# One output product moved ahead of a one-hot sum, and every row gather gated, in the last stage of a mixture-of-experts kernel

## The chip, the cores and the metric

The kernel runs on one core of a Trainium2 chip. The metric is the device time of one execution in microseconds (us), and of several executions the median. Engines: TensorE (PE; PEld are its weight loads), VectorE (DVE), ScalarE (ACT), GpSimd (POOL) and SyncE (SP), which only issues transfers.

## The reference

```
x = x + attention(layernorm(x), ctx)            # 512 tokens of 256
y = layernorm(x)
topk_idx, tw = gate(y)                          # 4 of 32 experts for a token
combine = zeros(T, E).at[t, topk_idx].add(tw)
routed = sum over experts e of combine[:, e] * (silu(y @ w1[e].T) * (y @ w3[e].T)) @ w2[e].T
out = x + routed + shared_swiglu(y)
```

Only the routed part matters here.

## The kernel before

Everything before about 220 us (attention, layer norm, gate, routing tables) is untouched. In the last stage the chosen token rows stand in 32 units of two blocks of 64 rows, handled in 16 pairs j = 0 to 15. TensorE takes a pair through four steps, each in its turn of one loop over j = 0 to 18 written out by hand:

- `x_rows` (line 708) transposes the gathered rows; ScalarE copies them out (968).
- `hidden` (719) multiplies by w1 and w3, 16 matmuls. ScalarE applies silu (981), and VectorE multiplies by the other half in `gated` (1314).
- `g_rows` (729) transposes that product, two transpositions; ScalarE copies it out in `gT_evict` (975).
- `out_rows` (740) multiplies by w2, 8 matmuls.

What becomes of an output depends on the pair. Pairs 0 to 9 are written to memory (`y_rows`), and GpSimd fetches them back for each token in 16 indirect transfers, `collect` (1418), each of 128 rows; VectorE adds each fetched tile to the result in `add_rows` (1298; the very last at 1367). I number these gathers 0 to 15. Pairs 10 to 15 don't go through memory. For each of them, p = 0 to 5, ScalarE writes a weighted copy (`weighted_high`, 991), VectorE the remainder of it (`weighted_rows`, 1289) and a one-hot matrix (`hot_rows`, 1278), and TensorE sums them into the token rows in `combine(p)` (685, 16 matmuls), the last in `combine_last` (696). VectorE adds these sums at the end (`add_sum`, 1358), and SyncE stores the four tiles (448).

Each engine works through its own list in order. VectorE's, at the end, is: `add_rows` of gathers 3 to 5, `gated(15)`, `hot_rows(5)`, `weighted_rows(4)`, gathers 6 to 8, `weighted_rows(5)`, gathers 9 to 11, gathers 12 and 13, `add_sum(0)` and `(1)`, gather 14, `add_sum(2)` and `(3)`, gather 15. The one-hot matrices and the weighted copies have two buffers, so that

```
                if p >= 2:
                    dve.wait_ge(acc_mm, p - 1)
```

stands in front of `hot_rows(p)`: `hot_rows(5)` waits until `combine(3)` has ended. `combine(p)` waits for `weighted_rows(p)`, and `g_rows(j)` for `gated(j)`. ScalarE's list at the end is: `gT_evict(14)`, silu of pair 15, `weighted_high(4)`, `gT_evict(15)`, `weighted_high(5)`.

A gather can be gated: `pool.wait_ge(*gates[i])` holds gather i until a count of TensorE's steps is reached. `hu_mm`, `gt_mm`, `yu_mm` count `hidden`, `g_rows` and `out_rows`, and `acc_mm` counts `combine`.

Of the kernel before, what the change touches and what calls it, by code (L numbers as in the profile page):

```python
# [46 lines left out]
NU = E  # L47
DIR = 12
# [17 lines left out]
def build(nc, x, ctx_kv, w_attn, w_gate, gate_bias, w_exp, rope_q, rope_x, rope_kv, ident_in, iota_in, w_sh, moe_c, iota_t, xn_dram, y_dram, out):  # L66
    with ExitStack() as stack:
# [3 lines left out]
        def sem(name):  # L71
            return stack.enter_context(nc.semaphore(name))
# [209 lines left out]
        gt_mm = sem("gt_mm"); gt_ev = sem("gt_ev"); yu_mm = sem("yu_mm"); yu_ev = sem("yu_ev")  # L282
# [38 lines left out]
        def out_count(u):  # L321

            return len([s for s in USED[:u + 1] if s not in AHEAD])
# [129 lines left out]
        def _(pe):  # L453
# [219 lines left out]
            def slot_weights():  # L673
                pe.wait_ge(w_one, 1)
                for k in range(NK):
                    mm = pe.matmul(sw_ps, f(one_r[:, k, :]), w_both[:, :, k, :], start=(k == 0), stop=(k == NK - 1))
                mm.then_inc(sw_mm, 1)
# [12 lines left out]
            def combine_last(p):  # L690
                pe.wait_ge(yu_ev, NG_U // 2 + p + 1)
                pe.wait_ge(oh_done, p + 1)
                for tt in range(TT):
                    for i in range(2):
                        for hl in range(2):
                            mm = pe.matmul(acc_ps[tt // 2][:, (tt % 2) * D:(tt % 2 + 1) * D],
                                           one_hot[:, p % 2, i, tt * P:(tt + 1) * P], yd[:, p % 2, i, hl, :],
                                           start=False, stop=(i == 1 and hl == 1 and tt % 2 == 1), skip_group_check=True)
                    if tt % 2 == 1:
                        mm.then_inc(acc_end, 1)  # L700

            def x_rows(j):
                if j >= 1:
                    pe.wait_ge(xt_ev, j)
                for u in (2 * j, 2 * j + 1):
                    pe.wait_ge(d_xg[u % XG], 16 * (u // XG + 1))
                    for dc in range(ND):
                        mm = pe.transpose(xt_ps[:, (u % 2 * ND + dc) * P:(u % 2 * ND + dc + 1) * P],  # L708
                                          xg[:, u % XG, dc * P:(dc + 1) * P], ident[:, :])
                mm.then_inc(xt_mm, 1)  # L710

            def hidden(j):
                pe.wait_ge(xt_ev, j + 1)
                if j >= 2:
                    pe.wait_ge(gu_done, j - 1)
                for u in (2 * j, 2 * j + 1):
                    for dc in range(ND):
                        for s, w in enumerate((over_w[u], u * WE)):
                            mm = pe.matmul(hu_ps[j % 2][s * BLK:(s + 1) * BLK, (u % 2) * 2 * I:(u % 2 + 1) * 2 * I],  # L719
                                           xTu[:, u % XS, dc, s * BLK:(s + 1) * BLK],  # L720
                                           wall[:, bass.ds(w + dc * 2 * I, 2 * I)], start=(dc == 0), stop=(dc == ND - 1))
                mm.then_inc(hu_mm, 1)

            def g_rows(j):
                pe.wait_ge(gu_done, j + 1)
                if j >= 1:
                    pe.wait_ge(gt_ev, j)
                for i in range(2):
                    mm = pe.transpose(gt_ps[:, i * P:(i + 1) * P], gu[:, i, :], ident[:, :])
                mm.then_inc(gt_mm, 1)  # L730

            def out_rows(j):
                pe.wait_ge(gt_ev, j + 1)
                if j == 0:
                    pe.wait_ge(sh_sum, TT)
                if j >= 2:
                    pe.wait_ge(yu_ev, j - 1)
                for u in (2 * j, 2 * j + 1):
                    for s, w in enumerate((over_w[u], u * WE)):
                        mm = pe.matmul(yu_ps[j % 2][s * BLK:(s + 1) * BLK, (u % 2) * D:(u % 2 + 1) * D],  # L740
                                       gTu[:, u % GS, s * BLK:(s + 1) * BLK],
                                       wall[:, bass.ds(w + 2 * ND * I, D)], start=True, stop=True)
                mm.then_inc(yu_mm, 1)
# [70 lines left out]
            for j in range(NU // 2 + 3):  # L814
                if j == 1:
                    hidden(0)
                if j < NU // 2:
                    x_rows(j)
                if j == 1:
                    slot_weights()  # L820
                if 2 <= j < NU // 2 + 2:
                    g_rows(j - 2)
                if 2 <= j <= NU // 2:
                    hidden(j - 1)
                if j == NU // 2 + 1:
                    out_rows(j - 2)
                if j == NU // 2 + 2:
                    combine_last(DIR // 2 - 1)
                elif j - 3 >= NG_U // 2:
                    combine(j - 3 - NG_U // 2)  # L830
                if 2 <= j < NU // 2 + 1:
                    out_rows(j - 2)


# [536 lines left out]
        @block.gpsimd  # L1371
        def _(pool):
            links = [0]

            def link(ins):

                links[0] += 1
                ins.then_inc(chain_p, 1)
                pool.wait_ge(chain_p, links[0])


            pool.wait_ge(d_kv, 32)
            hd = DC // 2
            for b in range(B):
                rows = slice(b * LC, (b + 1) * LC)
                pool.tensor_tensor(kvr[:, rows, 0, :], kv[:, rows, :], kvtab[:, :, 0, :], ALU.mult)
                pool.tensor_tensor(kvr[:, rows, 1, 0:hd], kv[:, rows, hd:DC], kvtab[:, :, 1, 0:hd], ALU.mult)
                link(pool.tensor_tensor(kvr[:, rows, 1, hd:DC], kv[:, rows, 0:hd], kvtab[:, :, 1, hd:DC], ALU.mult))
            link(pool.tensor_tensor(kvr[:, :, 0, :], kvr[:, :, 0, :], kvr[:, :, 1, :], ALU.add))
            pool.tensor_copy(kvr[:, :, 1, :], kvr[:, :, 0, :]).then_inc(kv_roped, 1)  # L1390

            def ropes(g, j):
                p = NPG * g + j
                for k in range(NQT):
                    if (p, k) in BY_DVE:
                        continue
                    pool.wait_ge(wk_out, out_count(use(g, "ABC"[k], j)))
                    if (g, "ABC"[k], j) != ALONE:
                        pool.wait_ge(q_swap, TURNED.index((g, "ABC"[k], j)) + 1)
                    rope_tile(pool, link, g, j, k, 2).then_inc(rope_p, 1)  # L1400
                    await_roped(pool, p, k)

            pool.wait_ge(d_rope, 16)
            for g in range(NG):
                for j in range(NPG):
                    ropes(g, j)
            pool.wait_ge(d_moe, 16)
            pool.tensor_copy(lower_b[:, :], lower).then_inc(const_b, 1)

            def gather(u):  # L1410
                if u >= XG:
                    pool.wait_ge(xt_mm, (u - XG) // 2 + 1)
                pool.indirect_dma_start(xg[:, u % XG, :], None, xn_dram, bass.IndirectOffsetOnAxis(idx[:, u:u + 1], 0)) \  # L1413
                    .then_inc(d_xg[u % XG], 16)

            def collect(tt, k):
                i = tt * TOPK + k
                pool.indirect_dma_start(y4[:, tt, k, :], None, y_dram, bass.IndirectOffsetOnAxis(place[:, i:i + 1], 0)) \  # L1418
                    .then_inc(d_y4[i], 16)

            for tt in range(TT):
                pool.wait_ge(d_xn[tt], 16)
            pool.wait_ge(idx_done, 2)
            for u in range(XG):
                gather(u)
            for u in range(XG, NU):
                gather(u)
            pool.wait_ge(placed, 1)
            for r in range(YS // 2):
                pool.wait_ge(d_yu[r], 16 * (NG_U // YS))  # L1430
            G2 = NG_U // 2
            gates = {1: (acc_mm, 1), 2: (yu_mm, G2 + 2), 3: (hu_mm, G2 + 4), 4: (acc_mm, 2), 5: (yu_mm, G2 + 3), 6: (hu_mm, G2 + 5),
                     7: (acc_mm, 3), 8: (yu_mm, G2 + 4), 9: (hu_mm, G2 + 6), 10: (acc_mm, 4), 11: (yu_mm, G2 + 5)}
            for i in range(NK):
                if i == 0:
                    pool.wait_ge(sw_mm, 1)
                if i in gates:
                    pool.wait_ge(*gates[i])
                collect(*divmod(i, TOPK))
# [96 lines left out]
```

## Time and profile before

| | |
|---|---|
| median of 3 executions | 302.06 us (301.9 to 302.15) |
| the profiled execution | 301.82 us |
| its span, first to last instruction | 299.5 us |
| PE busy | 282.5 us (94%) |
| DVE busy | 181.4 us (61%) |
| ACT busy | 156.4 us (52%) |
| POOL busy | 129.5 us (43%) |
| mean granted TensorE clock | 0.995 |

The span is what the trace covers; the profiled execution's own time is 2.32 us longer. Shares of busy time are means over stages with different limits. The stage that the change touches is the last 20 us.

### The profile page before, as it was taken

Reading aid. Unit: us, or ns where it says so; the run is one execution under the profiler, and the core shown is the slowest. Engines: PE = TensorE matmul, PEld = TensorE weight load, DVE = VectorE, ACT = ScalarE, POOL = GpSimd, SP = SyncE. Lnnn points to the kernel's source line nnn. Section 1 sums busy time; section 2 is a strip of 40 time slices with the busy share of each in tenths; the row PEclk is TensorE's granted clock in tenths of the full one; section 3 lists DMA queues with packets and bytes.
Section 4 is the critical chain, followed back from the end, with each engine's and each line's share of the span. In section 5 each row is a group of like instructions: output and inputs, shape, how many; then the busy total and the mean of one; then the engine's idle time right before and its main releaser. Section 6 shows DMA issues by size and latency. Waiting matters only on the chain.

```text
span 299.5 us, 5458 instructions
## 1 busy us (share of the span) xinstructions
PE 282.5 (94%) x1831; PEld 202.7 (68%) x1831; DVE 181.4 (61%) x434; ACT 156.4 (52%) x373; POOL 129.5 (43%) x121
## 2 busy tenths in 40 slices
PE   8988799999999999999999999978789999999982
PEld 6857568676777666787667777754567666676662
DVE  4877776576757777765854466158842233344676
ACT  2747469675785866777773355185212333343330
POOL 0656328791036770079940000000176555565572
PEclk9999999999999999999999999999999999999998
DMA  7962500001700001600039992402033544432234
GB/s 235 402 253 79 204 1 2 0 2 25 255 3 1 0 3 46 218 0 1 2 127 380 402 352 78 173 2 70 1 106 106 150 150 144 154 109 72 70 82 130
DMA packets 15994, 34.41 MB, mean 115 GB/s; under 512 B 2528, under 2 KB 8416, under 8 KB 15968
## 3 DMA queue, kind: packets, MB, share of 16 engines
q1 hardware_dynamic: 13664, 27.77, 26.0%
q0 software_dynamic: 2304, 6.29, 7.4%
q8 instruction: 16, 0.26, 0.4%
q14 instruction: 10, 0.08, 0.1%
HBM read 30.38 MB, written 3.67 MB: 114 GB/s over the span
## 4 chain that ended last, share of the span: by engine, by line
PE 85%; DVE 7%; DMA 2%; issue 2%; ACT 2%; POOL 1%; POOLq 0%; DVEq 0%; ACTq 0%
PE bank L719 10%; PE bank L612 10%; PE bank L595 9%; PE bank L583 5%; PE bank L562 5%; PE bank L584 4%; PE bank L740 4%; PE bank L456 4%; PE bank L458 4%; PE bank L457 4%; PE bank L505 3%; PE bank L708 3%; PE bank L537 3%; PE bank L685 3%; PE bank L540 3%; PE bank L463 2%
## 5 line engine op out<-in xcount | busy, mean ns | idle before, releaser
L1413 POOL DMA_INDIRECT rope<-xn_rows,idx x32 | 31.2, 974 | 83.3 <-DVE idx L1307 61.9
L893 ACT ACTIVATE prob<-bank,nmax 128x512 f32<-128x512 f32 x48 | 32.7, 685 | 38.9 <-DVE nmax L1097 38.9
L361 POOL TENSOR_TENSOR rtmp<-abuf,rope 128x512 f32<-128x512 f32 x20 | 25.7, 1284 | 60.4 <-PE bank L458 41.0
L1097 DVE TENSOR_REDUCE nmax<-bank 128x1 f32<-128x512 f32 x64 | 41.2, 685 | 8.7 <-PE bank L584 8.4
L719 PE MATMUL bank<-wall,nmat 128*64 (+1 forms) x256 | 31.2, 386 | 0.8 <-ACT nmat L968 0.8
L612 PE MATMUL bank<-pT,kvr 128*64 128x256 f32 x256 | 31.2, 386 | 0.0
L1115 DVE COPY pT<-bank 128x512 f32<-128x512 f32 x32 | 22.0, 687 | 13.1 <-PE bank L595 12.9
L583 PE MATMUL bank<-kdup,qsp 128*128 128x512 f32 x64 | 28.3, 442 | 1.2 <-ACT prob L893 1.2
L364 POOL TENSOR_TENSOR roped<-rtmp 128x512 f32<-128x512 f32 x20 | 25.9, 1295 | 1.6
L1314 DVE TENSOR_TENSOR kv<-bank,kv 128x256 f32<-128x256 f32 x16 | 6.8, 425 | 32.5 <-ACT kv L981 32.4
L595 PE MATMUL bank<-ident,prob 128*128 128x128 f32 x192 | 26.3, 273 | 0.0
L595 PEld LDWEIGHTS bank<-ident,prob 128*128 128x128 f32 x192 | 22.6, 141 | 4.9 <-issue 1.7
L362 POOL TENSOR_TENSOR rtmp<-abuf,rope 128x512 f32<-128x512 f32 x20 | 25.8, 1292 | 0.0
L584 PE MATMUL bank<-kdup,qsp 128*128 128x512 f32 x64 | 25.3, 395 | 0.0
L719 PEld LDWEIGHTS bank<-wall,nmat 128*64 128x64 f32 x256 | 16.9, 137 | 10.5 <-issue 3.5
L612 PEld LDWEIGHTS bank<-pT,kvr 128*64 128x64 f32 x256 | 16.9, 137 | 9.8 <-issue 2.8
L902 ACT COPY pT<-bank 128x512 f32<-128x512 f32 x32 | 18.9, 592 | 7.5 <-PE bank L595 7.2
L1061 DVE COPY abuf<-bank 64x512 f32<-64x512 f32 x20 | 13.7, 684 | 14.7 <-ACT abuf L867 14.4
L968 ACT COPY nmat<-bank 128x512 f32<-128x512 f32 x16 | 9.4, 585 | 23.3 <-PE bank L708 23.3
L1418 POOL DMA_INDIRECT ctT<-y_rows,place x16 | 16.3, 1017 | 10.3 <-PE bank L719 3.7
L456 PE MATMUL bank<-xnT,msplit 128*128 128x512 f32 x46 | 20.6, 447 | 0.0
L583 PEld LDWEIGHTS bank<-kdup,qsp 128*128 128x128 f32 x64 | 12.0, 188 | 9.2 <-issue 7.4
(217 smaller groups left out, 559.8 us busy)
## 6 DMA issues: line engine op xcount, KB each, us to landing
wall<-in_w_exp SPq DMA_DIRECT2D x32, 384.0 KB, 7.5
wring<-in_w_attn SPq DMA_DIRECT2D x16, 224.0 KB, 4.3
wring<-in_w_attn SPq DMA_DIRECT2D x4, 640.0 KB, 8.1
y_rows<-nmat SPq DMA_DIRECT2D x10, 256.0 KB, 2.1
wring<-in_w_attn SPq DMA_DIRECT2D x4, 512.0 KB, 7.0
rope<-in_rope_q SPq DMA_DIRECT2D x1, 768.0 KB, 7.0
x_sb<-in_x SPq DMA_DIRECT2D x1, 512.0 KB, 3.6
xn_rows<-xn SPq DMA_DIRECT2D x4, 128.0 KB, 1.7
```

The source lines that it names most:

```text
L361: eng.tensor_tensor(t0.rearrange("p (b s) -> p b s", b=B), own.rearrange("p (b s) -> p b s", b=B), cos, ALU.mult)
L362: link(eng.tensor_tensor(t1.rearrange("p (b s) -> p b s", b=B), other.rearrange("p (b s) -> p b s", b=B), sin, ALU.mult))
L364: return eng.tensor_tensor(roped[:, j, k, :], t0, t1, ALU.add)
L456: pe.matmul(out_ap, a_hi, b_hi, start=first, stop=False)
L583: pe.matmul(s_ps[t % 3][:, :], q, kdup[:, 0, b * L:(b + 1) * L], start=True, stop=False)
L584: pe.matmul(s_ps[t % 3][:, :], q, kdup[:, 1, b * L:(b + 1) * L], start=False, stop=True) \
L595: mm = pe.transpose(t_ps[t % 2][:, lc * P:(lc + 1) * P], probs[t % 4][:, lc * P:(lc + 1) * P], ident[:, :])
L612: mm = pe.matmul(pv_ps[hh * DC:(hh + 1) * DC, 0:S], kvr[:, b * LC + lc, 0, :], pT[:, (2 * n + hh) % PR, lc, :], start=(lc == 0), stop=(lc ...
L719: mm = pe.matmul(hu_ps[j % 2][s * BLK:(s + 1) * BLK, (u % 2) * 2 * I:(u % 2 + 1) * 2 * I], xTu[:, u % XS, dc, s * BLK:(s + 1) * BLK], wall ...
L893: act.activation(probs[t % 4], s_ps[t % 3][:, :], ACT.Exp, bias=nmax[:, t:t + 1], accum_out=psum_e[:, t:t + 1]).then_inc(s_exp, 1)
L1097: dve.tensor_reduce(nmax[:, t:t + 1], s_ps[t % 3][:, :], AX.X, ALU.max, negate=True).then_inc(s_max, 1)
L1413: pool.indirect_dma_start(xg[:, u % XG, :], None, xn_dram, bass.IndirectOffsetOnAxis(idx[:, u:u + 1], 0)) \
```

## The change

`combine(3)` leaves the turn j = 16 and stands in the turn j = 17, between `g_rows(15)` and `out_rows(15)`. `out_rows(14)` thereby follows `hidden(15)` at once. No matmul, copy or transfer is added or taken away, and no other engine's list changes order. In GpSimd's list each gather from 1 to 15 has a gate; before, 12 to 15 had none. Three gates count transpositions (`gt_mm`). G2 is 10.

```diff
-                if j == NU // 2 + 1:
+                if j == NU // 2:
                     out_rows(j - 2)
-                if j == NU // 2 + 2:
+                elif j == NU // 2 + 1:
+                    combine(DIR // 2 - 3)
+                    out_rows(j - 2)
+                    combine(DIR // 2 - 2)
+                elif j == NU // 2 + 2:
                     combine_last(DIR // 2 - 1)
                 elif j - 3 >= NG_U // 2:
                     combine(j - 3 - NG_U // 2)
-                if 2 <= j < NU // 2 + 1:
+                if 2 <= j < NU // 2:
                     out_rows(j - 2)
...
-            gates = {1: (acc_mm, 1), 2: (yu_mm, G2 + 2), 3: (hu_mm, G2 + 4), 4: (acc_mm, 2), 5: (yu_mm, G2 + 3), 6: (hu_mm, G2 + 5),
-                     7: (acc_mm, 3), 8: (yu_mm, G2 + 4), 9: (hu_mm, G2 + 6), 10: (acc_mm, 4), 11: (yu_mm, G2 + 5)}
+            gates = {1: (acc_mm, 1), 2: (yu_mm, G2 + 2), 3: (hu_mm, G2 + 4), 4: (acc_mm, 2), 5: (yu_mm, G2 + 3), 6: (gt_mm, G2 + 4),
+                     7: (hu_mm, G2 + 5), 8: (acc_mm, 3), 9: (yu_mm, G2 + 4), 10: (gt_mm, G2 + 5), 11: (hu_mm, G2 + 6),
+                     12: (yu_mm, G2 + 5), 13: (gt_mm, G2 + 6), 14: (acc_mm, 4), 15: (yu_mm, G2 + 6)}
```

TensorE's order at the end, in steps:

```
before: g_rows(14) hidden(15) combine(3) out_rows(14) g_rows(15) out_rows(15) combine(4) combine_last(5)
after:  g_rows(14) hidden(15) out_rows(14) g_rows(15) combine(3) out_rows(15) combine(4) combine_last(5)
```

## Rows read from the trace of the kernel before

**Rows 1.** Timeline of TensorE, 282 to 294 us: start, duration, line, operation, idle before.

```profile
282.27 0.44 PE L729 MATMUL bank<-ident,kv 128*128 128x128 f32 x2
282.64 1.95 PE L719 MATMUL bank<-wall,nmat 128*64 x16
284.52 2.17 PE L685 MATMUL bank<-xnT,kdup 128*128 128x256 f32 x16
286.62 1.08 PE L740 MATMUL bank<-wall,ctmp 128*64 x8
287.63 0.44 PE L729 MATMUL bank<-ident,kv 128*128 128x128 f32 x2
288.99 1.08 PE L740 MATMUL bank<-wall,ctmp 128*64 x8 [0.92 <-ACT ctmp L975]
290.00 2.18 PE L685 MATMUL bank<-xnT,kdup 128*128 128x256 f32 x16
292.02 2.16 PE L696 MATMUL bank<-xnT,kdup 128*128 128x256 f32 x16
```

**Rows 2.** Timeline of VectorE, 284 us to the end.

```profile
284.15 1.52 DVE L1298 SCALAR_TENSOR_TENSOR x_sb<-ctT,topw,x_sb 128x256 f32<-128x256 f32 x3
285.70 0.42 DVE L1314 TENSOR_TENSOR kv<-bank,kv 128x256 f32<-128x256 f32 x1
286.73 0.88 DVE L1278 TENSOR_SCALAR kdup<-rtmp,tokf 128x512 fp32r<-128x512 f32 x2 [0.60 <-PE bank L685]
288.72 0.88 DVE L1289 SCALAR_TENSOR_TENSOR xnT<-bank,wslot,xnT 128x256 fp32r<-128x256 f32 x2 [1.11 <-ACT xnT L991]
289.51 1.52 DVE L1298 SCALAR_TENSOR_TENSOR x_sb<-ctT,topw,x_sb 128x256 f32<-128x256 f32 x3
291.08 0.88 DVE L1289 SCALAR_TENSOR_TENSOR xnT<-bank,wslot,xnT 128x256 fp32r<-128x256 f32 x2
291.88 1.52 DVE L1298 SCALAR_TENSOR_TENSOR x_sb<-ctT,topw,x_sb 128x256 f32<-128x256 f32 x3
293.91 1.01 DVE L1298 SCALAR_TENSOR_TENSOR x_sb<-ctT,topw,x_sb 128x256 f32<-128x256 f32 x2 [0.51 <-DMA ctT<-y_rows,place]
294.95 0.76 DVE L1358 TENSOR_TENSOR x_sb<-bank,x_sb 128x256 f32<-128x256 f32 x2
...
296.13 0.76 DVE L1358 TENSOR_TENSOR x_sb<-bank,x_sb 128x256 f32<-128x256 f32 x2
296.92 0.48 DVE L1367 SCALAR_TENSOR_TENSOR x_sb<-ctT,topw,x_sb 128x256 f32<-128x256 f32 x1
```

**Rows 3.** Timeline of ScalarE, 287 to 289 us.

```profile
287.75 0.84 ACT L991 ACTIVATE xnT<-bank,wslot 128x256 fp32r<-128x256 f32 x2 [2.73 <-PE bank L740]
288.48 0.37 ACT L975 COPY ctmp<-bank 128x256 f32<-128x256 f32 x1
```

**Rows 4.** Timeline of GpSimd, 284 us to the end: gathers 9, 10, 12 and 15.

```profile
284.87 1.10 POOL L1418 DMA_INDIRECT ctT<-y_rows,place  x1 [0.95 <-PE bank L719]
286.96 1.07 POOL L1418 DMA_INDIRECT ctT<-y_rows,place  x1 [0.99 <-PE bank L685]
...
289.59 1.22 POOL L1418 DMA_INDIRECT ctT<-y_rows,place  x1 [0.30 <-issue]
...
293.62 0.95 POOL L1418 DMA_INDIRECT ctT<-y_rows,place  x1 [0.30 <-issue]
```

**Rows 5.** Line 1418, all 16 gathers: time from issue to landing.

```profile
DMA to landing us min/median/max: 2.7/2.9/4.2
```

**Rows 6.** Timeline, 194 to 196 us: a VectorE result that TensorE waits for.

```profile
194.67 0.42 DVE L1122 TENSOR_TENSOR ctT<-bank,ctmp 128x256 f32<-128x256 f32 x1 [4.67 <-ACT ctmp L909]
...
195.24 1.10 PE L562 MATMUL bank<-nmat,ctT 128*128 128x256 f32 x4 [0.71 <-DVE ctT L1122]
```

**Rows 7.** Timeline of TensorE's weight loads, `combine(3)`.

```profile
284.52 1.97 PEld L685 LDWEIGHTS bank<-xnT,kdup 128*128 128x128 f32 x16 [0.38 <-DVE xnT L1289]
```

**Rows 8.** Busy times by stretch: PE, PEld, DVE, ACT, POOL, granted clock, DMA share, GB/s.

```profile
289.00:294.20 5.20, 5.18 (x40) 4.42 (x40) 4.49 (x11) 0.84 (x2) 3.98 (x5) 1.00 0.41 103
```

## The prediction

> **What bounds the kernel now.** I read the shares of busy time first (TensorE 94%), then the timeline of each engine over the last 16 us, because only there does the order change. The reader is to see in the timeline of TensorE that it works without a gap until `g_rows(15)` and then waits once, 0.92 us, for ScalarE's copy of the transposed product, before `out_rows(15)` [rows 1]. That is the wait the change fills. Then look at who works last: TensorE ends at 292.02 + 2.16 = 294.18 us, but VectorE goes on to 297.40, and the store of the last tile ends the run [rows 1, 2]. So the end is set by VectorE's list. From 288.72, where `weighted_rows(4)` starts, VectorE has one idle stretch only: 0.51 us before the add of gather 12, which has not landed [rows 2]. The gather began at 289.59 and the landing of such a gather takes 2.7 to 4.2 us [rows 4, 5]. A gain for TensorE counts only if it lets this list of VectorE start sooner. I therefore ask of each edit when `weighted_rows(4)` starts, and what idle time is left behind it.
>
> **The moved sum, step by step.** Everything to the end of `hidden(15)` stays, since no earlier step moves: the next step of TensorE starts at 284.52 [rows 1].
>
> 1. `out_rows(14)` takes that place. Its input was copied out before (ScalarE's copy of pair 14 came a whole `hidden` earlier). It occupies TensorE until 284.52 + 1.01 = 285.53, 1.01 being the distance from 286.62 to 287.63 [rows 1].
> 2. `g_rows(15)` needs `gated(15)`. This one is held on VectorE by the three adds in front of it, which end at 285.67, so it runs from 285.70 to 286.12 as before [rows 2]. Before, 3.1 us of `combine(3)` and `out_rows(14)` covered silu and product; now `out_rows(14)` alone does. For the hand-over from VectorE to TensorE I take 0.15 us: a result that ended at 194.67 + 0.42 = 195.09 released a matmul at 195.24 [rows 6]. `g_rows(15)` starts at 286.27; TensorE waits 0.74 us. A wait appears where there was none.
> 3. Two transpositions take 282.64 - 282.27 = 0.37 us [rows 1], and `combine(3)` starts at 286.64. Unseen is a one-hot sum right behind transpositions: its weight loads start 0.38 us after those of the step before when that is a `hidden` [rows 7], and that gap is already inside the distances between steps. The bounds for the turn are 0.37 and 0.37 + 0.38 = 0.75; I take 0.37, since the `hidden` in the row also follows two transpositions directly.
> 4. `hot_rows(5)` must wait for `combine(3)`, which used its buffer. Before, the sum started at 284.52 and `hot_rows(5)` at 286.73, 2.21 later [rows 1, 2]. Now it starts at 286.64 + 2.21 = 288.85, which is 2.12 us later than before.
> 5. `weighted_rows(4)` is queued behind it. Before, it started at 288.72 because ScalarE's weighted copy came at 287.75, released by `out_rows(14)` at 286.62 [rows 1, 2, 3]. Now that product starts at 284.52 and the copy is there near 286.5, so only `hot_rows(5)` holds it. Two such instructions occupy 0.79 us (288.72 to 289.51) [rows 2]; the other bound is their full 0.88 plus a hand-over of 0.05. I take 0.80: 289.65, against 288.72 before, so **+0.93 us**.
> 6. `combine(4)` wants `weighted_rows(4)`, which ends at 289.65 + 0.88 = 290.53, while TensorE is free at 288.74 + 1.01 = 289.75. `combine(4)` starts at 290.68 after a second new wait of 0.9 us. `weighted_rows(5)` comes 0.79 + 1.57 us after `weighted_rows(4)` (289.51 to 291.08 for the adds), at 292.01, ends at 292.89, and `combine_last` starts at 293.04 and ends near 295.2. `add_sum(2)`, 1.18 us after the pair of sums at 294.95 in the old list, comes at about 296.6 [rows 2], so TensorE stays off the path by 1.4 us.
>
> The wait that is filled: `out_rows(15)` follows `combine(3)` at 286.64 + 2.10 = 288.74 instead of 288.99 [rows 1]. TensorE wins 0.25 us there, but its next consumer is behind VectorE's list.
>
> At step 5 one page can be held against a row. The rows show the next VectorE instructions starting at 289.51 while the two before are still shown until 289.60 [rows 2]. The Trainium skill ("VectorE: DVE Perf Modes", The DRAIN you can't avoid) says that the next operation doesn't start until the pipeline has emptied; by that rule the term would be 0.88 and the sum 0.08 more. The trace does not agree, and I keep the row.
>
> **The gates.** The gathers are issued by GpSimd, 0.95 us each and 0.30 between [rows 4]. Gather 12, which VectorE waits for now, is gated on `out_rows(14)`, and that step moves forward by 2.1 us. Gather 11's gate is the end of `hidden(15)`, which released GpSimd at 284.87 [rows 4]. With 1.25 us for each in a full queue, gather 11 starts by about 285.5, 12 by 286.8, 13 by 288.0. Gather 14 is gated on `combine(3)`: 286.64 + 2.44 = 289.08 (before, that gate opened from 284.52 to 286.96 [rows 1, 4]), and the queue makes it 289.3. Gather 15 is gated on `out_rows(15)`, open about 290.1, so it starts by 290.5, 3.1 us sooner than the 293.62 of before [rows 4]. With the slowest landing, 4.2 us [rows 5], gather 12 is there at 291.0 for an add at 294.4, gather 14 at 293.5 for one at about 296.1, gather 15 at 294.7 for one at 297.4. No row is waited for. The gap on VectorE from 291.88 + 1.55 = 293.43 to 293.91 goes: **-0.48 us** [rows 2]. The lower bound is also -0.48 (there is no more idle time), the upper 0, if some row is late after all. Four more waits in GpSimd's list are hidden by its idle time.
>
> **The sum.** +0.93 - 0.48 = +0.45 us at the last add, 297.37 against 296.92. The store behind it is the same. The profiled execution would go from 301.82 to 302.27 us; it lies 0.24 below the median of 302.06, so the median goes to 302.51, +0.15%. That is within 0.2% (0.60 us), about what a measurement of this kernel can tell from no change.
>
> **The rivals.**
>
> - *A hand-over larger than its row* (slower, other side). Each hundredth between `gated(15)` and `hot_rows(5)` reaches the end undiminished. From 0.15 us more the result is beyond 0.2%. The turn at its upper bound (+0.38) and full drains (+0.13) give +0.96: 303.0 us. For it: the order transposition, one-hot sum is nowhere in the trace, and the idle row wait no longer absorbs anything. Against: every distance between other steps repeats to a hundredth. Chance 0.21.
> - *TensorE and the rows were the bound* (faster). If the one-hot rows did not hold `weighted_rows(4)`, the 0.25 us of TensorE and the 0.48 us of the row wait would both be won: -0.73, 301.3 us. It decides if `hot_rows(5)` could start by 287.7. For it: both waits are real rows [rows 1, 2]. Against: the semaphore wait in front of `hot_rows`, and its 0.60 us idle behind `combine(3)` [rows 2]. Chance 0.10.
> - *The two halves cancel* (no change to 0.2 us). Silu and `gated(15)` come sooner than the row, because the three adds in front of it (held only by their gathers and VectorE's list) shift; at most 0.44 us, to where it would start after silu. 302.1 us. Chance 0.05.
> - *The clock falls* (slower). TensorE gets three waits of up to 0.9 us in 7 us; in the stretch with the present waits the granted clock is 1.00, the 2.4 GHz level [rows 8]. At half that, `combine_last` would take 2.16 us more, end at 297.4, and push the last sums and the end by about 0.9 beyond the forecast: 303.4 us. It decides only if the clock falls before 293. Chance 0.04.
>
> **How the numbers follow.** The forecast as worked out has 0.60, with its own range of 302.3 to 302.75. Together with the cancelling case, within 0.2% has 0.65; slower 0.21 + 0.04 = 0.25; faster 0.10. The range leaves out part of the faster rival and of the clock: 301.6 to 303.1.
>
> **What the profile after would show.** `out_rows(14)` directly behind `hidden(15)`; a wait of about 0.7 us at `g_rows(15)` for VectorE; none at `out_rows(15)`; a wait of about 0.9 us at `combine(4)` for line 1289; VectorE idle some 2.7 us before line 1278 and not at all from there to the end; gather 15 starting near 290.5; no wait of line 1298 for a transfer. Wrong would be: `hot_rows(5)` well before 288.8, a remaining wait for a gather, or `combine_last` ending after 296.5.

## The result, and the profile after

The changed kernel was measured at a median of 304.08 us (302.05 to 304.87, 20 executions) beside 302.2 us of the kernel before (301.67 to 303.5, 20 executions): ratio 1.0046, 95% interval 1.0033 to 1.0059. It is slower, by some 1.4 us going by the ratio, where +0.15% was forecast, and the median lies above the range of 301.6 to 303.1 us. The medians differ by more, 1.88 us, because the executions of the changed kernel fall into two groups: thirteen took 303.99 to 304.87 us, six took 302.05 to 302.84, and one took 303.28. Three more measurements, on three chips, gave 1.0013, 1.0019 and 1.0009, with medians of 302.46 to 302.68 us; the median of the six is 302.46. Both the excess of the first measurement and the small loss of the others have to be explained.

The profiled execution took 304.11 us, so it is one of the thirteen, with a span of 301.8 us against 299.5. No other execution of this measurement has a trace. Timeline of TensorE after, against [rows 1]:

```profile
282.83 1.95 PE L719 MATMUL bank<-wall,nmat 128*64 x16
284.61 1.03 PE L740 MATMUL bank<-wall,ctmp 128*64 x8
286.37 0.44 PE L729 MATMUL bank<-ident,kv 128*128 128x128 f32 x2 [0.73 <-DVE kv L1318]
286.56 2.15 PE L685 MATMUL bank<-xnT,kdup 128*128 128x256 f32 x16
288.64 1.08 PE L740 MATMUL bank<-wall,ctmp 128*64 x8
292.39 2.91 PE L685 MATMUL bank<-xnT,kdup 128*128 128x256 f32 x16 [2.66 <-DVE xnT L1293]
295.10 2.87 PE L696 MATMUL bank<-xnT,kdup 128*128 128x256 f32 x16
```

Timeline of VectorE after, against [rows 2] (lines are four higher):

```profile
285.89 0.42 DVE L1318 TENSOR_TENSOR kv<-bank,kv 128x256 f32<-128x256 f32 x1
290.67 0.88 DVE L1282 TENSOR_SCALAR kdup<-rtmp,tokf 128x512 fp32r<-128x512 f32 x2 [4.35 <-remote]
291.46 0.87 DVE L1293 SCALAR_TENSOR_TENSOR xnT<-bank,wslot,xnT 128x256 fp32r<-128x256 f32 x2
...
294.60 2.56 DVE L1302 SCALAR_TENSOR_TENSOR x_sb<-ctT,topw,x_sb 128x256 f32<-128x256 f32 x5
...
298.38 0.76 DVE L1362 TENSOR_TENSOR x_sb<-bank,x_sb 128x256 f32<-128x256 f32 x2
299.17 0.48 DVE L1371 SCALAR_TENSOR_TENSOR x_sb<-ctT,topw,x_sb 128x256 f32<-128x256 f32 x1
```

Timeline of ScalarE after, against [rows 3]:

```profile
286.31 0.84 ACT L995 ACTIVATE xnT<-bank,wslot 128x256 fp32r<-128x256 f32 x2 [1.08 <-PE bank L740]
287.73 0.37 ACT L979 COPY ctmp<-bank 128x256 f32<-128x256 f32 x1 [0.58 <-PE bank L729]
290.76 0.84 ACT L995 ACTIVATE xnT<-bank,wslot 128x256 fp32r<-128x256 f32 x2 [2.66 <-PE bank L740]
```

Timeline of GpSimd after, gathers 14 and 15, against [rows 4]:

```profile
290.90 1.07 POOL L1422 DMA_INDIRECT ctT<-y_rows,place  x1 [1.51 <-remote]
292.27 0.95 POOL L1422 DMA_INDIRECT ctT<-y_rows,place  x1 [0.31 <-issue]
```

The reader is to see the forecast's shape, and one number that is wrong. `out_rows(14)` follows `hidden(15)`; `g_rows(15)` waits 0.73 us for `gated(15)`; `out_rows(15)` waits for nothing; VectorE does not stop from line 1282 to the end, and no add waits for a gather. But `hot_rows(5)` (line 1282) starts 4.11 us behind the start of `combine(3)` (286.56 to 290.67). It had been 2.21 [rows 1, 2]. The timeline calls the releaser "remote": it names no instruction whose recorded end would fit.

What is late is the signal, not the work. The copy that waits for `out_rows(15)` starts at 290.76, 0.09 us behind `hot_rows(5)`. That product follows `combine(3)` and takes TensorE 1.08 us. Had TensorE really ended `combine(3)` at 290.6, the product could not have ended 0.1 us later. GpSimd's gather 14, which waits for the same sum, starts at 290.90, so it isn't VectorE that was slow. Earlier signals are late too: `out_rows(14)` to ScalarE's copy 1.70 us (284.61 to 286.31), before 1.13 (286.62 to 287.75); `g_rows(15)` to its copy 1.36 us (286.37 to 287.73), where the changed kernel measured again (e5) has 0.48.

I place VectorE's last add by its distance from the start of `hidden(15)`, which leaves out whatever happened earlier. Before it is 296.92 - 282.64 = 14.28 us, forecast 14.73, after 299.17 - 282.83 = 16.34. Of the 2.29 us by which the profiled execution is longer (301.82 to 304.11), 2.06 us lie in this distance and 0.19 us before it. The distance carries the rest of the study.

### The profile page after: what moved, and what is told of

Same layout as the page of the kernel before. It is cut to its first block, busy times and chain, and to the rows that moved or that the text cites. A ratio compares the mean times of both kernels' runs of the same rounds, so it can differ in the third digit from the quotient of the medians.

```text
span 301.8 us, 5458 instructions
## 1 busy us (share of the span) xinstructions
PE 283.7 (94%) x1831; PEld 204.2 (68%) x1831; DVE 181.4 (60%) x434; ACT 156.5 (52%) x373; POOL 129.7 (43%) x121
## 4 chain that ended last, share of the span: by engine, by line
PE 81%; DVE 9%; issue 3%; ACT 2%; POOL 2%; another core or an unknown queue 1%; DMA 1%; DVEq 0%; POOLq 0%; ACTq 0%
PE bank L612 10%; PE bank L595 9%; PE bank L719 9%; PE bank L583 5%; PE bank L562 5%; PE bank L584 4%; PE bank L740 4%; PE bank L456 4%; PE bank L458 4%; PE bank L457 4%; PE bank L505 3%; PE bank L537 3%; PE bank L540 3%; PE bank L708 3%; PE bank L463 2%
```

## The experiments

Four groups, e1 to e4, e5 to e8, e9 to e12 and e13 to e15, each on a chip of its own with its own executions of the kernel before (medians 303.07, 302.09, 301.99 and 302.29 us). Ratios are to those, with the 95% interval. The interval holds the scatter within one measurement and not what a change of chip does: the changed kernel alone went from 1.0009 to 1.0046. "Stage" is the distance just defined. "Signals" says whether the trace has a signal of TensorE from `hidden(14)` on that is late by more than 0.3 us.

| run | ratio | interval | stage us | signals |
|---|---|---|---|---|
| before | 1 | | 14.28 | on time |
| changed kernel, first measurement | 1.0046 | 1.0033 to 1.0059 | 16.34 | late |
| e1 new order, old gates | 1.0039 | 1.0025 to 1.0053 | 15.75 | on time |
| e2 old order, new gates | 0.9971 | 0.9957 to 0.9986 | 13.81 | late |
| e3 changed, wait filled | 1.0027 | 1.0009 to 1.0044 | 16.04 | late |
| e4 changed, hot_rows(5) later | 1.0001 | 0.9986 to 1.0017 | 14.62 | late |
| e5 changed | 1.0013 | 1.0004 to 1.0023 | 14.65 | on time |
| e6 sum before transpositions | 0.9978 | 0.9968 to 0.9988 | 13.45 | on time |
| e7 changed, gathers 9 to 15 held back | 1.0310 | 1.0281 to 1.0339 | 22.85 | on time |
| e8 old order, new gates, adds first | 0.9956 | 0.9942 to 0.9970 | 13.02 | on time |
| e9 changed | 1.0019 | 1.0006 to 1.0032 | 14.65 | on time |
| e10 new order, old gates | 1.0063 | 1.0038 to 1.0087 | 15.61 | on time |
| e11 old order, new gates | 0.9992 | 0.9977 to 1.0006 | 14.00 | on time |
| e12 e6 with adds first | 0.9942 | 0.9919 to 0.9965 | 12.41 | on time |
| e13 changed | 1.0009 | 0.9995 to 1.0022 | 14.66 | on time |
| e14 as e6 | 0.9968 | 0.9952 to 0.9984 | 13.46 | on time |
| e15 as e4 | 0.9981 | 0.9965 to 0.9996 | 13.29 | on time |

**e1 and e10: the new order alone** (the diff of `gates` undone).

> The new order of TensorE with the old gates. Theory (late signals come with the order): in the changed kernel hot_rows(5) started at 290.67 us, 1.8 us later than the 2.21 us that combine(3) took before, in one execution. If the order is the cause of the whole loss, this kernel is about as slow as the changed one, 302.5 to 304.1 us. Rival (the gates are the cause, because the gathers run beside the end of combine(3)): this kernel stays at the forecast's +0.45 us, plus 0.48 us where the ungated gathers 12 to 15 are late again: at most 303.0 us, with hot_rows(5) 2.2 us behind the start of combine(3).

> The new order with the old gates again. By the rows: +0.93 us for the later start of VectorE's list, and gathers 10 to 15 some 2 us later behind the gate on combine(3), so waits for gathers 10 to 13 in VectorE's list of 1.3 us in place of 0.5: together +1.5 us, ratio 1.005 (a measurement on one chip gave 1.0039). If the old gates did not matter: as the changed kernel of the same call.

The order alone costs 0.4 to 0.6% (medians 303.93 and 304.05 us). On the one chip where both were measured that is more than the whole change, 1.0063 (6 executions) beside 1.0019. e10, VectorE's adds of gathers 11 to 13, and the gate that causes them:

```profile
293.97 0.48 DVE L1302 SCALAR_TENSOR_TENSOR x_sb<-ctT,topw,x_sb 128x256 f32<-128x256 f32 x1 [0.18 <-DMA ctT<-y_rows,place]
295.31 0.48 DVE L1302 SCALAR_TENSOR_TENSOR x_sb<-ctT,topw,x_sb 128x256 f32<-128x256 f32 x1 [0.86 <-DMA ctT<-y_rows,place]
296.00 0.48 DVE L1302 SCALAR_TENSOR_TENSOR x_sb<-ctT,topw,x_sb 128x256 f32<-128x256 f32 x1 [0.20 <-DMA ctT<-y_rows,place]
```

```profile
285.14 1.10 POOL L1422 DMA_INDIRECT ctT<-y_rows,place  x1 [0.95 <-PE bank L719]
289.08 1.07 POOL L1422 DMA_INDIRECT ctT<-y_rows,place  x1 [2.84 <-PE bank L685]
```

In the old gates gather 10 waits for `combine(3)`, which now starts 3.74 us behind `hidden(15)` instead of 1.88, so 1.9 us later, and 11 to 15 queue behind it: 1.24 us of row waits. Its stage of 15.61 is 0.96 above e9's, so beside the new order the new gates are worth 0.96 us. The e1 trace shows `hot_rows(5)` on time, 2.19 us behind `combine(3)`, and 1.32 us of idle time in front of the adds of gathers 11 to 13. So the order alone did not make signals late in this execution; that late signals don't need the new order is shown by e2, next.

**e2 and e11: the new gates alone.**

> The old order of TensorE with the new gates. By the forecast: within 0.3 us of before, since no row is on the path other than gather 12 (0.48 us), which can only come later with a gate that opens at 287.7. Rival (the gates delay TensorE's signals or the rows): slower than before by 1 us or more.

> The new gates with the old order again. By the rows: the row wait of 0.48 us is gone and nothing else changes, ratio 0.9984; where signals are late, combine(3) in front of g_rows(15) hides a late signal of hidden(15), and the first measurement gave 0.9971. If the gain of the gates is only 0.48 us, the ratio lies between 0.9975 and 0.9990 on a chip with signals on time.

The stage is 0.47 us shorter than before in e2 and 0.28 in e11, where gather 13 still keeps VectorE waiting 0.23 us. e2's ratio is a greater gain than that; I have no row for the surplus. The kernel before was itself 0.8 to 1.1 us slower on this chip than on the other three (303.07 us beside 301.99 to 302.29), and it has no trace there, so the surplus may lie in what e2 is compared with. In e2 a signal is late as well. TensorE, ScalarE and VectorE of e2:

```profile
283.43 1.95 PE L719 MATMUL bank<-wall,nmat 128*64 x16
...
288.42 0.44 PE L729 MATMUL bank<-ident,kv 128*128 128x128 f32 x2
```

```profile
287.04 0.38 ACT L981 ACTIVATE kv<-bank 128x256 f32<-128x256 f32 x1 [2.67 <-remote]
```

```profile
287.51 0.42 DVE L1314 TENSOR_TENSOR kv<-bank,kv 128x256 f32<-128x256 f32 x1 [0.96 <-ACT kv L981]
```

Silu of pair 15 starts 3.61 us behind `hidden(15)`, and 1.99 is usual. Yet `g_rows(15)` starts with no wait: the old order has `combine(3)` and `out_rows(14)` between. In this trace the lateness costs the old order nothing: the stage is the 14.28 us of before less the row wait. A late signal of `combine(3)` was not seen in the old order.

The lateness starts before any step that the change moves. The step one pair earlier, `hidden(14)`, in e2:

```profile
278.07 1.95 PE L719 MATMUL bank<-wall,nmat 128*64 x16
280.91 0.39 ACT L981 ACTIVATE kv<-bank 128x256 f32<-128x256 f32 x1 [1.94 <-PE bank L719]
```

Silu of pair 14 starts 2.84 us behind it; e3 and e4 have 2.86 and 2.88, the other traces 1.99 to 2.08. But e1, the one trace of this chip with the old gates, is on time, and e2 to e4, all with the new gates, are late. That the new gates take part in it, on this chip, is a rival that these runs leave standing.

**e3: the wait filled.**

```diff
+                if j == NU // 2 + 1:
+                    for _ in range(4):
+                        pe.matmul(bank[3][:, 0:P], ident[:, :], ident[:, :], start=True, stop=True)
                 if 2 <= j < NU // 2 + 2:
                     g_rows(j - 2)
```

> The changed kernel with four 128-column fp32 matmuls of no use (0.74 us at 0.185 us each) in TensorE's wait in front of g_rows(15). If the late signals of the changed kernel come from TensorE having stood idle there, they go: hot_rows(5) 2.2 us behind the start of combine(3), 302.5 us. If they don't depend on that idle time: as the changed kernel, near 304 us.

The kernel stays as slow as the changed one in the first measurement (303.82 us, stage 16.04), but by other signals. TensorE, ScalarE and VectorE of e3:

```profile
283.13 1.95 PE L719 MATMUL bank<-wall,nmat 128*64 x16
284.90 1.03 PE L740 MATMUL bank<-wall,ctmp 128*64 x8
285.87 1.16 PE L823 MATMUL bank<-ident 128*128 128x128 f32 x8
```

```profile
286.76 0.38 ACT L988 ACTIVATE kv<-bank 128x256 f32<-128x256 f32 x1 [2.79 <-remote]
```

```profile
287.91 2.15 PE L685 MATMUL bank<-xnT,kdup 128*128 128x256 f32 x16
290.09 0.98 DVE L1285 TENSOR_SCALAR kdup<-rtmp,tokf 128x512 fp32r<-128x512 f32 x2 [2.43 <-PE bank L685]
```

The signal of `hidden(15)` comes 1.6 us late before TensorE has waited for anything in this stretch, and that of `out_rows(15)` reaches ScalarE after 2.84 us (289.99 to 292.83) instead of 1.13. But the signal that was late in the first trace, that of `combine(3)`, is on time: `hot_rows(5)` starts 2.18 us behind it. (The 4 matmuls stand in the trace as 8: each fp32 matmul has two records. The 16 and 8 told for `hidden` and `out_rows` are records too; the code issues 8 and 4.) So late signals come without idle time of TensorE in front of them; for the signal of `combine(3)` alone, one execution doesn't exclude it.

**e5, e9, e13: the changed kernel again.**

> The changed kernel once more, so that it stands on one chip beside the next three. Theory (the moved sum exposes TensorE's late signals, and costs 0.93 us even without one): 0.3 to 0.5% slower than before, with executions spread over some 2 us as in the first measurement (302.05 to 304.87). Rival (the first measurement was the chip's): within 0.2% of before.

> The changed kernel a third time. So far it was 0.46% slower where its trace had late signals of TensorE, and 0.13% where it had none. Theory (the chip, not the program, decides whether TensorE's signals come late, and the new order pays for it): if the traces of this call show signals that are on time, the ratio is near 1.0013; if they show late ones, near 1.004. Rival (the difference was chance): a ratio near 1.003 whatever the traces show.

> The changed kernel a fourth time. Theory (a structural loss of 0.13 to 0.19%, and more only where TensorE's signals are late): ratio 1.001 to 1.002 if the trace shows hot_rows(5) starting 2.2 us behind combine(3); 1.003 to 1.005 if the signals of this chip are late. Rival (the surplus was chance in the first measurement): 1.001 to 1.002 in either case.

TensorE and VectorE of e5:

```profile
282.37 1.95 PE L719 MATMUL bank<-wall,nmat 128*64 x16
284.15 1.03 PE L740 MATMUL bank<-wall,ctmp 128*64 x8
285.96 0.44 PE L729 MATMUL bank<-ident,kv 128*128 128x128 f32 x2 [0.78 <-DVE kv L1318]
286.16 2.16 PE L685 MATMUL bank<-xnT,kdup 128*128 128x256 f32 x16
```

```profile
288.35 1.06 DVE L1282 TENSOR_SCALAR kdup<-rtmp,tokf 128x512 fp32r<-128x512 f32 x2 [2.44 <-PE bank L685]
289.33 0.86 DVE L1293 SCALAR_TENSOR_TENSOR xnT<-bank,wslot,xnT 128x256 fp32r<-128x256 f32 x2
...
297.02 0.48 DVE L1371 SCALAR_TENSOR_TENSOR x_sb<-ctT,topw,x_sb 128x256 f32<-128x256 f32 x1
```

`hot_rows(5)` is 2.19 us behind `combine(3)`; the stage is 14.65, 14.65 and 14.66 in the three traces, +0.37 us on before. None has a late signal, and the ratios are 1.0009 to 1.0019. The 0.3 to 0.5% expected of e5 missed; its rival, within 0.2%, is what came. Three on-time traces can't exclude the rival of chance, but the first trace's surplus is one signal, and in all three that signal is on time.

**e6 and e14: the sum before the transpositions.**

```diff
+                if j == NU // 2 + 1:
+                    combine(DIR // 2 - 3)
                 if 2 <= j < NU // 2 + 2:
                     g_rows(j - 2)
...
                 elif j == NU // 2 + 1:
-                    combine(DIR // 2 - 3)
                     out_rows(j - 2)
```

> The changed kernel with combine(3) one step earlier: out_rows(14), combine(3), g_rows(15), out_rows(15). Theory (the loss is that combine(3) stands behind g_rows(15), and so behind silu and gated(15), while hot_rows(5) and all of VectorE's list wait for it): combine(3) starts 1.0 us behind the end of hidden(15), hot_rows(5) 2.2 us later, VectorE's idle time falls from 2.7 to some 1.6 us, weighted_rows(4) comes about 0.2 us earlier than before the change, and with the row wait of 0.48 us gone the kernel is 0.5 to 0.9 us faster than before, about as the gates alone (0.9971). Rival (out_rows(14) right behind hidden(15), or the new order as a whole, makes TensorE's signals late): as slow as the changed kernel, above 1.003.

> combine(3) in front of g_rows(15), again. With signals on time, as measured: 0.9978. If this chip's signals are late, combine(3) covers a late signal of hidden(15), as it does in the old order, and the ratio stays at 0.997 to 0.998 while the changed kernel goes to 1.003 or more. Rival (late signals cost both orders the same): this one rises by as much as the changed kernel.

Faster than before by 0.2 to 0.3% each time; 1.2 us shorter in the stage than the changed kernel, by the place of the 16 matmuls of `combine(3)` alone. VectorE of e6:

```profile
288.07 0.88 DVE L1283 TENSOR_SCALAR kdup<-rtmp,tokf 128x512 fp32r<-128x512 f32 x2 [1.42 <-PE bank L685]
...
296.56 0.48 DVE L1372 SCALAR_TENSOR_TENSOR x_sb<-ctT,topw,x_sb 128x256 f32<-128x256 f32 x1
```

The wait in front of `hot_rows(5)` is 1.42 us, not 2.44. e14 got no late signal, so whether this order also hides one wasn't seen.

**e4 and e15: VectorE's list.** `hot_rows(5)` behind `weighted_rows(4)` and the adds of gathers 6 to 8:

```diff
-                if j - 2 >= NG_U // 2 - 1 and j - 1 - NG_U // 2 < DIR // 2:
+                if j - 2 >= NG_U // 2 - 1 and j < NU // 2:
                     hot_rows(j - 1 - NG_U // 2)
...
                     add_rows(PACE * p, PACE * (p + 1))
+                    if j == NU // 2:
+                        hot_rows(DIR // 2 - 1)
```

> The changed kernel, with hot_rows(5) on VectorE moved behind weighted_rows(4) and the adds of gathers 6 to 8, so that these don't stand behind the wait for combine(3). Theory (VectorE's list held by that wait is the loss): VectorE works through 2.3 us of its list during the wait, weighted_rows(5) follows the signal of combine(3) by 0.9 us plus ScalarE's copy, and the end comes 1.5 to 2 us before that of the changed kernel: 301 us if the signal is on time, below 302.5 if it is late. Rival (the late signal alone sets the end, whatever stands behind): no gain over the changed kernel.

> The changed kernel with hot_rows(5) moved behind weighted_rows(4) and the adds of gathers 6 to 8. With signals on time VectorE does 2.3 us of its list during the wait of 2.44 us, hot_rows(5) still starts 2.2 us behind combine(3), and weighted_rows(5) then waits for ScalarE's copy until about 1.9 us behind hot_rows(5). The last add comes 1.3 to 1.6 us sooner than in the changed kernel: ratio 0.996 to 0.997 to before. If the list behind the wait is not what sets the end: no gain over the changed kernel.

VectorE of e15:

```profile
287.43 0.88 DVE L1293 SCALAR_TENSOR_TENSOR xnT<-bank,wslot,xnT 128x256 fp32r<-128x256 f32 x2 [0.34 <-ACT xnT L995]
288.23 1.51 DVE L1302 SCALAR_TENSOR_TENSOR x_sb<-ctT,topw,x_sb 128x256 f32<-128x256 f32 x3
289.77 1.02 DVE L1282 TENSOR_SCALAR kdup<-rtmp,tokf 128x512 fp32r<-128x512 f32 x2
291.53 0.88 DVE L1293 SCALAR_TENSOR_TENSOR xnT<-bank,wslot,xnT 128x256 fp32r<-128x256 f32 x2 [0.73 <-ACT xnT L995]
```

TensorE's order is the changed kernel's, but the list no longer stands behind the wait: 1.37 us off the stage, ratio 0.9981 beside 1.0009. The gain in the ratio, 0.85 us, is less than I expected. e4, with signals of `hidden(15)` and others late, only equals before, and its 302.86 us misses the expected 302.5; but its stage is 1.42 us shorter than that of e3 on the same chip, where `hidden(15)` was late by the same 1.64 us.

**e7: gathers 9 to 15 held until TensorE has ended.**

> The changed kernel with gathers 9 to 15 held until combine_last has ended. The end comes some 8 to 10 us later, since seven gathers of 1.25 us follow, so its total time tells nothing of the change. What it tells: if the gathers that run beside the end of TensorE's work make its signals late, every signal from hidden(15) to combine_last comes as in the rows of before (hidden 1.98 us after its start, out_rows 1.10, g_rows 0.46, combine 2.18), and the executions lie within some 0.5 us of each other. If the signals are late whatever the gathers do, at least one is late by more than 0.3 us here as well, and the executions spread over 1.5 us or more.

310.89 us (310.52 to 312.81, 4 executions). All signals were on time, but so were those of the other three kernels on that chip, gathers and all, and the executions spread over 2.3 us where 0.5 was expected with them. It tells nothing of the cause, so the gathers remain a rival.

**e8 and e12: the adds first.** e8 puts the adds of gathers 6 to 8 and 9 to 11 in front of `weighted_rows(4)` and `(5)`, in the old order with new gates. e12 does it on e6, there those of 6 to 8 in front of `hot_rows(5)`.

> The old order of TensorE with the new gates, and on VectorE the adds of gathers 6 to 8 ahead of weighted_rows(4), those of 9 to 11 ahead of weighted_rows(5). Theory (VectorE's list sets the end, and its wait for ScalarE's copy, 0.65 to 1.11 us in front of weighted_rows(4), is the next thing to fill): the waits shrink by about 1 us, combine(4) starts at most 0.3 us later, and the kernel is 0.7 to 1.2 us faster than the gates alone, ratio about 0.993 to before. Rival (TensorE's end sets the time once the rows are early): combine(4) and combine_last wait for the later weighted_rows, and it gains nothing over the gates alone, 0.997.

> combine(3) in front of g_rows(15), the new gates, and on VectorE the adds of gathers 6 to 8 in front of hot_rows(5) (they fill its 1.42 us wait), those of 9 to 11 in front of weighted_rows(5). Theory (the end is VectorE's list and its idle time behind TensorE's sums): the last add starts 12.4 us behind the start of hidden(15), where it was 14.28 before, 13.45 with the sum moved alone and 13.02 with the adds first alone: 1.7 us faster than before, ratio 0.993 to 0.995. Rival (TensorE's end takes over, since combine_last ends 2.2 us behind weighted_rows(5)): no better than the adds first alone, 0.9956.

e8's stage is 13.02 us, 0.79 us shorter than the gates alone in e2 and 0.98 than in e11; its ratio of 0.9956 (6 executions) is a smaller gain than the 0.993 expected. Its sums at the end wait 0.47 us for TensorE.

VectorE of e12:

```profile
286.79 1.51 DVE L1303 SCALAR_TENSOR_TENSOR x_sb<-ctT,topw,x_sb 128x256 f32<-128x256 f32 x3
288.37 0.88 DVE L1283 TENSOR_SCALAR kdup<-rtmp,tokf 128x512 fp32r<-128x512 f32 x2
...
293.76 0.76 DVE L1366 TENSOR_TENSOR x_sb<-bank,x_sb 128x256 f32<-128x256 f32 x2 [0.47 <-PE bank L696]
...
295.74 0.48 DVE L1375 SCALAR_TENSOR_TENSOR x_sb<-ctT,topw,x_sb 128x256 f32<-128x256 f32 x1
```

The adds fill the wait, the stage is 12.41 us as expected, and the kernel is 0.58% faster than before by the ratio (medians 300.49 us, of 5 executions, and 301.99). The one idle time left behind `hot_rows(5)`, 0.47 us, is for TensorE's last sum, so I take TensorE for the next bound; no run tested it.

## Why the prediction was wrong, and where it was right

The step that failed is step 4: `hot_rows(5)` at 2.21 us behind the start of `combine(3)`. I took that distance as a constant and, against the first rival, wrote that every distance between other steps repeats to a hundredth. In the trace after it was 4.11 us. From the 14.73 us forecast, the stage follows: +1.90 for that signal, -0.18 for the turn behind the transpositions (0.19 instead of 0.37), -0.09 for an earlier `g_rows(15)` (3.54 us behind `hidden(15)`, not 3.63), -0.01 for step 5, which is 16.35 against 16.34 measured. The first rival named the right place, between `gated(15)` and `hot_rows(5)`, and the right rule, that each hundredth there reaches the end, but with other causes and at less than half the price: +0.96 us over before in all, where the stage grew by 2.06.

Without late signals the sum was right: +0.37 us in the stage in three traces for +0.45, ratios of 1.0009 to 1.0019 for a forecast of 1.0015. The turn in step 3 was over-priced by 0.17 us in e5, which step 5 gave back there (0.98 instead of 0.80); the rest are hundredths.

- Step 1: ScalarE's copy of pair 14 was there, but it had ended at 283.49 (283.12 + 0.37), 1.03 us before it was needed and not a whole `hidden`. It changed nothing.
- Step 2, the new wait at `g_rows(15)`: 0.74 us forecast; 0.73 and 0.78 measured.
- Step 5, the row that was preferred to the page: `weighted_rows(4)` starts 0.79 us behind `hot_rows(5)` in the trace after (290.67 to 291.46), as the row had it, and not 0.88 as by the sentence I took from the Trainium skill ("VectorE: DVE Perf Modes", The DRAIN you can't avoid). The same paragraph adds that a next operation that is not held starts earlier, so the page is not at odds with the row; I had read it without its exception. In e5 it is 0.98, but there the pair of `hot_rows(5)` itself takes 1.06 us, so the next one again starts 0.08 us before its end.
- Step 6, TensorE off the path: it ended at 297.97 for a sum at 298.38, in spite of a clock that I had as a rival. That is past the 296.5 which I had named as a sign of being wrong, and it came from the late start of `combine(4)`; in e5 `combine_last` ended at 294.78. Busy times by stretch after (columns as [rows 8]):

```profile
292.00:293.00 1.00, 0.61 (x5) 0.61 (x6) 0.96 (x3) 0.00 (x0) 0.73 (x1) 1.00 0.32 78
293.00:294.00 1.00, 1.00 (x9) 1.00 (x8) 0.93 (x3) 0.00 (x0) 0.22 (x1) 0.74 0.39 102
294.00:295.00 1.00, 1.00 (x7) 1.00 (x6) 1.00 (x3) 0.00 (x0) 0.00 (x0) 0.50 0.29 90
```

  The granted clock fell to 0.50, the 1.2 GHz level, behind TensorE's wait of 2.66 us; `combine(4)` took 2.91 us instead of 2.18. It cost nothing here, because VectorE was later still.
- The gates: no add waited, as forecast, though gather 15 started at 292.27, behind the late signal, and not by 290.5 (290.53 in e5), and -0.48 us was right for the old order in e2 (-0.47; in e11, with a row wait left, -0.28). I did not work out what the old gates would do under the new order. They cost 0.96 us there (e10 beside e9), so the two halves of the change belong together.
- The faster rival failed for the reason given. e6 and e15 show what it asked for: let `hot_rows(5)` start sooner, or take it out of the way, and the change gains.

Shown by the trace after: the late signal makes the excess of the profiled execution over the forecast, and the place of `combine(3)` exposes VectorE's list to it. That the whole 0.46% of the first measurement comes from it is argued, not shown. For it: the executions fall into two groups, the lower one at the 302.46 us of e5, and the medians of the groups, 302.46 and 304.62 us, lie 2.2 us apart, where the stage of the late trace is 1.7 us longer than the on-time ones. But only one of the twenty has a trace.

Not settled: why TensorE's signals come late. It doesn't need the new order (e2 has it in the old), nor a step that the change moves (`hidden(14)` is late in e2 to e4), nor idle time of TensorE in front (e3). The four traces with it come from two measurements, the first one and e2 to e4; the eleven traces e5 to e15, on three chips other than that of e2 to e4, have none in this stage. That points to the chip or its state, but not to something fixed, since executions of the first measurement fall into two groups. The new gates are the rival that no run excludes: every late trace has them, and e1, on the chip of e2 to e4 with the old gates, is on time. Against them as the only cause stand the nine on-time traces with all the new gates on those three chips.

## What to carry to other kernels

Filling a wait of the busiest engine gains nothing when another engine's list sets the end; follow what the moved work releases, and ask what stands in that list behind the wait for it. Here 16 matmuls one step earlier (e6), or one entry of VectorE's list put behind two others (e15), turned the loss into a gain, and adds moved into the waits as well (e12) made it 0.58%. Gates that count steps are part of the order: move a step and each gate on it moves its whole queue. And leave slack where a hand-over stands on the path, since its distance in one trace can be an optimistic one.

## What the runs showed of the hardware

In four traces of seventeen TensorE's semaphore signals came late by up to 1.9 us while its matmuls went on at their pace, and in one of them two signals, of steps of which the second takes 1.08 us, arrived 0.09 us apart. Every engine that waited was hit (290.67, 290.76 and 290.90 us in the trace after). Whoever explains such a gap by the matmuls' ends, which are modelled, finds a releaser called "remote". In one execution this made a stage of 16.34 us out of one that takes 14.65 with all signals on time. What sets it off is open.
